# First attention of a two-layer kernel: causal mask of the transposed scores by a minimum on VectorE instead of mask matmuls on TensorE

## What is computed

```
attn = jnp.einsum('bhqd,bhkd->bhqk', q, k) / math.sqrt(HEAD_DIM)
attn = attn + alibi_bias(seq_len, N_HEADS)[None] + causal_mask(seq_len)[None, None]
attn = jax.nn.softmax(attn, axis=-1)
y = jnp.einsum('bhqk,bhkd->bhqd', attn, v)
x = x + (y @ W_o) * silu(ffn(xn))      # written short; the FFN has a Walsh-Hadamard transform
```

## Time and profile before

| | |
|---|---|
| median of three runs | 1381.1 us |
| profiled execution, span from first to last instruction | 1408.8 us |
| TensorE matmuls busy | 1272.3 us |
| VectorE busy | 846.9 us |
| ScalarE busy | 597.1 us |
| GpSimd busy | 473.7 us |
| mean granted TensorE clock | 0.965 |
| first layer | about 18 to 455 us of the span |

### The profile page before, as it was taken

The page is one execution under the profiler, slowest core; times in us unless marked ns, Lnnn a source line. Parts: engine busy times, 40 slices in busy tenths (PEclk is TensorE's granted clock), DMA queues, the critical chain, the costliest instruction groups (busy, mean ns, idle before and its releaser), DMA issues.

```text
span 1408.8 us, 26582 instructions
## 1 busy us (share of the span) xinstructions
PE 1272.3 (90%) x9326; PEld 1107.9 (79%) x9327; DVE 846.9 (60%) x1731; ACT 597.1 (42%) x1351; POOL 473.7 (34%) x488
## 2 busy tenths in 40 slices
PE   5699979979998879989897899899999999999996
PEld 4588878768777766667666888889998999898996
DVE  4647547557556553333346777767665676667685
ACT  3333323323323334444453444454554555455542
POOL 0112332332331320000007878644343444343442
PEclk9799999999999999999999999999999999999998
DMA  5744314223101943323223121200000000000001
GB/s 196 282 177 154 134 59 150 100 97 143 46 31 36 340 174 94 93 82 97 89 76 116 53 76 46 75 1 31 2 1 31 1 31 1 1 1 1 1 24 38
DMA packets 63658, 112.07 MB, mean 80 GB/s; under 512 B 6977, under 2 KB 36033, under 8 KB 62017
## 3 DMA queue, kind: packets, MB, share of 16 engines
q1 hardware_dynamic: 57408, 93.79, 19.0%
q0 software_dynamic: 6144, 16.79, 3.6%
HBM read 49.86 MB, written 60.69 MB: 78 GB/s over the span
## 4 chain that ended last, share of the span: by engine, by line
PE 80%; DVE 8%; issue 7%; ACT 3%; POOL 1%; DMA 1%; another core or an unknown queue 1%; SPq 0%; ACTq 0%; DVEq 0%; POOLq 0%
PE bank L705 7%; PE six L722 6%; PE six L830 4%; PE bank L792 4%; PE bank L794 4%; PE bank L793 4%; PE bank L392 4%; PE bank L393 3%; PE bank L394 3%; PE bank L867 2%; PE bank L865 2%; PE bank L866 2%; PE bank L804 2%; PE six L844 2%; PE bank L805 2%
## 5 line engine op out<-in xcount | busy, mean ns | idle before, releaser
L1822 POOL TENSOR_TENSOR rstd<-msq,half_pow 128x8 f32<-128x8 f32 x64 | 105.5, 1648 | 163.1 <-DVE msq L1633 162.7
L1149 ACT ACTIVATE pT<-six,rstd 128x256 f32<-128x256 f32 x128 | 60.9, 476 | 213.6 <-PE six L831 213.6
L1759 POOL TENSOR_TENSOR hid_l<-hid,hid_h 128x256 fp32r<-128x256 f32 x64 | 48.2, 753 | 243.4 <-ACT hid_h L963 243.4
L1834 POOL TENSOR_TENSOR pT<-pT,tri_mul 128x512 f32<-128x512 f32 x64 | 84.3, 1318 | 130.8 <-ACT pT L1195 129.9
L1233 DVE TENSOR_TENSOR yT1l<-six,yT1h 128x512 fp32r<-128x512 f32 x64 | 44.3, 692 | 135.0 <-ACT yT1h L1200 135.0
L705 PE MATMUL bank<-experts,xT 128*128 x316 | 109.5, 470 | 17.5 <-issue 16.8
L1626 DVE TENSOR_TENSOR sq<-xs 128x512 f32<-128x512 f32 x128 | 102.1, 797 | 23.3 <-ACT xs L1168 23.3
L792 PE MATMUL bank<-bw_h,xT1h 128*128 128x512 f32 x256 | 106.9, 418 | 6.5 <-issue 6.5
L794 PE MATMUL bank<-bw_l,xT1h 128*128 128x512 f32 x256 | 101.8, 398 | 0.0
L793 PE MATMUL bank<-bw_h,xT1l 128*128 128x512 f32 x256 | 101.1, 395 | 0.0
L830 PE MATMUL six<-qT,kT 128*128 128x256 f32 x256 | 78.5, 388 | 18.7 <-issue 15.4
(11 more groups left out here) (282 smaller groups left out, 4068.4 us busy)
## 6 DMA issues: line engine op xcount, KB each, us to landing
cells_scratch<-zeros SPq DMA_DIRECT2D x8, 4352.0 KB, 14.9
xg<-cells_scratch SPq DMA_DIRECT2D x79, 128.0 KB, 2.0
cells_scratch<-y SPq DMA_DIRECT2D x79, 128.0 KB, 1.7
experts<-pack_experts_dram SPq DMA_DIRECT2D x16, 608.0 KB
raw<-pack_attn_dram SPq DMA_DIRECT2D x8, 1024.0 KB, 4.9
raw<-pack_w_dram SPq DMA_DIRECT2D x2, 1024.0 KB, 4.8
xT_scratch<-xT1h_c SPq DMA_DIRECT2D x8, 256.0 KB, 2.0
xT_scratch<-xT1l_c SPq DMA_DIRECT2D x8, 256.0 KB, 2.6
```

The source lines that it names most:

```text
L1822: pool.tensor_tensor(out=rstd[:, r, :], in0=msq[:, r, :], in1=half_pow[:], op=ALU.pow).then_inc(rstd_sb, 1)
L1834: pool.tensor_tensor(out=p, in0=p, in1=tri_mul[:].unsqueeze(1).unsqueeze(1).to_broadcast([P, 2, 2, P]), op=ALU.mult).then_inc(masked1, 1)
```

## The change

`scores_T` loses its four mask matmuls; its score matmuls now start their banks themselves. A new VectorE step `causal(b, g)` takes the minimum of the two diagonal blocks of each head with `tri_cap`, in place in PSUM, in two instructions of two heads each (128 x 512). `tri_cap` is fp32, 1e30 where the key may be seen and -1e30 where not. `exps` waits for the half it reads instead of for `scores_T`. `causal` is called at four places of VectorE's batch.

```diff
-                for h in range(GH):
-                    pe.matmul(six[:, h, 0:T], ident_b[:], tri_addT[:].rearrange("p c k -> p (c k)"),
-                              start=True, stop=False, skip_group_check=True)
                 for h in range(GH):
                     r = slice(h * VW, (h + 1) * VW)
-                    pe.matmul(six[:, h, P:3 * P], kA[r, g, 0:P], qB[r, g, :], start=False, stop=True, skip_group_check=True)
+                    pe.matmul(six[:, h, P:3 * P], kA[r, g, 0:P], qB[r, g, :], start=True, stop=True, skip_group_check=True)
                 for h in range(GH):
                     r = slice(h * VW, (h + 1) * VW)
-                    last = pe.matmul(six[:, h, 0:P], kA[r, g, P:T], qB[r, g, P:T], start=False, stop=True,
+                    last = pe.matmul(six[:, h, 0:P], kA[r, g, P:T], qB[r, g, P:T], start=True, stop=True,
                                      skip_group_check=True)
                 last.then_inc(sT0_ps, 1)
...
             def exps(b, g):
-                act.wait_ge(sT0_ps, 4 * b + g + 1)
                 after(act, y0_ps, 4 * b + g - 1)
                 for h in (0, 2):
+                    act.wait_ge(causal0, 8 * b + 2 * g + h // 2 + 1)
                     last = act.activation(pT0[:, g % 2, h:h + 2, :], six[:, h:h + 2, 0:3 * P], ACT.Exp)
                 last.then_inc(exp0, 1)
...
+            def causal(b, g):
+
+                dve.wait_ge(sT0_ps, 4 * b + g + 1)
+                for h in (0, 2):
+                    s = six[:, h:h + 2, 0:T].rearrange("p h (c q) -> p h c q", c=2)
+                    dve.tensor_tensor(out=s, in0=s, in1=tri_cap[:].unsqueeze(1).unsqueeze(1).to_broadcast([P, 2, 2, P]),
+                                      op=ALU.min).then_inc(causal0, 1)
...
                 if not first:
                     out_T(t)
+                    causal(b, 0)
                     gate_s(t, banks[0][:, :])
                 if first:
+                    causal(b, 0)
                     ffn_lo(2, w1_l, w1_h)
                     ffn_lo(3, w3_l, w3_h)
...
                 hidden(b, 1)
                 beside(3)
+                causal(b, 1)
                 if not first:
                     stats(t, st1, mv1, ve1, st1_sb, mv1_sb, ve1_sb, b)
...
                 hidden(b, 3)
                 heads_out(b, 1)
+                causal(b, 2)
                 if not final:
                     stats(b + 1, st0, mv0, ve0, st0_sb, mv0_sb, ve0_sb)
...
                 hidden(b, 5)
                 heads_out(b, 2)
+                causal(b, 3)
                 if not first:
                     router(t, 0)
...
-            dve.tensor_scalar(out=tri_addT[:], in0=tri_mul[:].unsqueeze(1).to_broadcast([P, 2, P]), scalar1=1.0,
-                              scalar2=1e30, op0=ALU.subtract, op1=ALU.mult)
+            dve.tensor_scalar(out=tri_cap[:], in0=tri_mul[:], scalar1=0.5, scalar2=2e30, op0=ALU.subtract, op1=ALU.mult)
```

More of the change, by code:

```diff
@@ L103, in build @@
         hadamard_r = sa("hadamard_r", [P, P], F32R)
-        ident_b, tri_add, tri_addT = sa("ident_b", [P, P], BF16), sa("tri_add", [P, 2, P], BF16), sa("tri_addT", [P, 2, P], BF16)
+        ident_b, tri_add, tri_cap = sa("ident_b", [P, P], BF16), sa("tri_add", [P, 2, P], BF16), sa("tri_cap", [P, P])
         q_row, k_rows = sa("q_row", [P, 1]), sa("k_rows", [P, NG, T])
@@ L198, in build @@
             "down_ps"))
-        yt0_sb, yq0_ps = sem("yt0_sb"), sem("yq0_ps")
+        yt0_sb, yq0_ps, causal0 = sem("yt0_sb"), sem("yq0_ps"), sem("causal0")
         xT1_ps, lgT_ps, lg_ps, pos_ps = (sem(n) for n in ("xT1_ps", "lgT_ps", "lg_ps", "pos_ps"))
@@ L441, in scores_T @@
                 for h in range(GH):
-                    pe.matmul(six[:, h, 0:T], ident_b[:], tri_addT[:].rearrange("p c k -> p (c k)"),
-                              start=True, stop=False, skip_group_check=True)
+                    r = slice(h * VW, (h + 1) * VW)
+                    pe.matmul(six[:, h, P:3 * P], kA[r, g, 0:P], qB[r, g, :], start=True, stop=True, skip_group_check=True)
                 for h in range(GH):
                     r = slice(h * VW, (h + 1) * VW)
-                    pe.matmul(six[:, h, P:3 * P], kA[r, g, 0:P], qB[r, g, :], start=False, stop=True, skip_group_check=True)
-                for h in range(GH):
-                    r = slice(h * VW, (h + 1) * VW)
-                    last = pe.matmul(six[:, h, 0:P], kA[r, g, P:T], qB[r, g, P:T], start=False, stop=True,
+                    last = pe.matmul(six[:, h, 0:P], kA[r, g, P:T], qB[r, g, P:T], start=True, stop=True,
                                      skip_group_check=True)
```

## The result

The changed kernel took 1395.97 us (median of 4 runs, 1395.54 to 1396.85), the kernel before 1377.95 us on the same chip (4 runs, 1373.42 to 1381.57): ratio 1.0134, 95% interval [1.0101, 1.0168]. It is slower, by 18 us where 9.6 were forecast; the time lies in the forecast's range of 1377 to 1404 us.

The account below looks back on a forecast made before the run. TensorE was taken as the bound by a few tenths only, VectorE in batch 0; 3 x 0.5 + 1.0 + 3 x 1.4 + 2.9 = 9.6 us slower made 1391 us, range 1377 to 1404.

Parts of the forecast that it names:

- the chain: First attention, each group: the minimum between scores_T and the exponentials ends them about 0.7 us later; likeliest case, slower, chance 0.44.
- The halves: The two VectorE minimum instructions per group: 0.69 us each, starting when VectorE leaves hidden(1) or heads_out(1), not at scores_T's end.
- PE waits before L421 of groups 2 and 3: TensorE before the scores of groups 2 and 3: idle 0.5 to 0.7 us, released by ScalarE's exponentials.
- maxima_T: TensorE's L435 behind maxima(2) in group 1: L1288 and L1289 end late, so it waits 0.3 us.
- The router's path: Group 3: r_th comes 0.5 us later, delaying hidden(6); TensorE's wait before norm_T0 grows from 0.93 to near 1.5 us.
- The ordinary batch: Batches 1, 3 and 5: each 0.5 us longer, not 1.8 shorter.
- Batch 0: First batch, VectorE-bound by butterflies: hidden(2) 3.1 us late, passed on to the hadamard matmul; less 0.2, +2.9 us.
- The held batches: Batches 2, 4, 6 and 7, with VectorE waiting on "remote": +1.0 us in batch 2, +1.4 in each other.
- rival A: Whole kernel: no difference that can be told, within 6.9 us; with weaker holds 6.4 us more, 1387.5; chance 0.34.
- Rival B: TensorE in the first attention: faster, its time returns as exponentials stay covered; at most 14.7 us, 1366; chance 0.10.
- Rival D: TensorE after the wait before norm_T0: clock falls, 1.6 us in each of six batches, 10 more, 1401; chance 0.12.
- The base: Whole kernel: traced span 1408.8 us is 27.7 above the runs' 1381.1; this difference was carried over to the forecast.

Follow-up runs that it names:

- e8: The changed kernel itself, unedited, traced again on one chip with the kernel before: 1415.80 us, ratio 1.0062 to the kernel before.
- e9: The kernel before, unedited, traced again on the same chip as the changed kernel: 1406.36 us, ratio 0.9991.
- e10: The kernel before without any mask (no matmuls, no minimum; exponentials scaled by 0.25) and with TensorE's batch loop written out: 1382.90 us, ratio 0.9843.
- e5: The kernel before with TensorE's loop over batches 1 to 6 written out, mask matmuls kept: 1396.45 us, ratio 0.9897 to the kernel before.
- e0: The kernel before, unedited, run for a second profile: 1396.86 us, ratio 1.000.
- e2: The changed kernel with the mask matmuls put back beside the minimum: 1421.30 us, ratio 1.0136 to the kernel before.
- e1: The kernel before without any mask (no mask matmuls, no minimum; exponentials scaled by 0.25), loop kept: 1396.72 us, ratio 0.9985.
- e3: The changed kernel with VectorE's order changed in batch 0 alone, causal(1) ahead of the last butterflies: 1414.50 us, ratio 1.0108 to the kernel before.
- e6: No mask matmuls or minimum; VectorE multiplies the exponentials by a triangle in SBUF, loop kept: 1403.99 us, ratio 0.9979 to the kernel before.
- e11: The changed kernel, unedited, run a third time on a third chip: 1414.53 us, ratio 1.0076 to the kernel before.

## Why the prediction was right, and where it was short

**The sign and the chain: right.** The steps it named show in the rows above. The instruction is 0.69 us. The halves start at the end of hidden(1) and of heads_out(1). PE waits before L421 of groups 2 and 3 in batches 1 to 7, 0.43 to 0.49 in each, for 0.5 to 0.7 forecast. maxima_T waits 0.20 for 0.3. The router's path, the step that passes the rest to the end of the batch (compare):

```profile
281.07 0.65 PE L402 MATMUL bank<-ident,xn 128*128 128x128 f32 x4 [1.65 <-DVE hid L1312]
```

is 1.65 for "near 1.5". The ordinary batch is 0.30 longer, forecast 0.5.

**Batch 0: right.** Timeline of DVE, ACT and PE, against the earlier trace rows:

```profile
40.63 1.29 DVE L1301 TENSOR_TENSOR six<-six,tri_cap 128x512 f32<-128x512 f32 x2
41.36 1.51 ACT L939 ACTIVATE pT<-six 128x768 f32<-128x768 f32 x2 [3.69 <-DVE six L1301]
43.48 0.42 DVE L1308 SCALAR_TENSOR_TENSOR th<-th,bank 128x256 f32<-128x256 f32 x1 [1.56 <-ACT th L955]
...
50.95 0.80 PE L606 MATMUL bank<-w_h,hadamard_r 128*128 128x512 f32 x1 [11.98 <-DVE w_l L1230]
```

DVE is idle for the forecast's 1.6 us (1.56) behind exps(1). Counted from the first scores, the hadamard matmul is 2.9 us later in e8 than in e9 (50.29 - 18.22 against 48.22 - 19.05), and the batch 3.1; between the two first traces it is 2.0 and 2.3.

**The held batches: near in sum where there are holds, not one by one.** Without the jumps' longer waits, batches 2, 4, 6 and 7 gave 0.95, 1.28, 1.00 and 0.62 for 1.0, 1.4, 1.4 and 1.4 in the pair e8 and e9. Batches 3 and 5 gave 2.1 and 0.0 for 0.5. They were taken as ordinary, but they have holds in these traces (PE waits 2.90 us for qA before L520 in batch 3 of e8), and had them in the trace of before, where the prediction looked only at DVE's gate:

```profile
196.43 0.61 PE L442 MATMUL six<-tri_addT,ident_b 128*128 128x256 bf16 x4 [3.57 <-issue]
...
305.66 0.61 PE L442 MATMUL six<-tri_addT,ident_b 128*128 128x256 bf16 x4 [3.69 <-issue]
```

The holds move between executions; a price per batch isn't to be had from one. That 9.35 comes so near to 9.6 is in part luck: batch 5's 0.0 holds 1.4 us of a slow start that e9 had and e8 had not. And the changed kernel's own trace, on the chip of the result, has no hold in any of batches 2 to 7. There the chain can be estimated as batch 0's 3.1 and 7 x 0.3, some 5 us, near rival A's 6.4 for a kernel with weak holds.

**What was missing: the jump.** The sum ran over groups and batches and took PE's loop as free. The trace of before had its wait, and it was not read as something that a change of PE's code can move:

```profile
186.11 0.61 PE L421 MATMUL six<-tri_add,ident_b 128*128 128x256 bf16 x4 [2.38 <-issue]
...
295.23 0.61 PE L421 MATMUL six<-tri_add,ident_b 128*128 128x256 bf16 x4 [2.35 <-issue]
```

It became 5.1 to 5.8 each: +5.5 us for the two in the pair e8 and e9, which with the chain's 9.35 makes 14.9. Rival B's mechanism (PE's time comes back) is real too, 11.3 of 14.7 us in e10 against e5; with the loop the jumps eat a good part of it, and with the minimum the exponentials' delay eats the rest.

**Rival D (the clock) was near in the price, 1.6 us for 1.4 to 2.9, and wrong about the place.** After the 1.65 us of idle time before norm_T0 the clock stays up: the changed kernel's batches 1 and 6, with that wait in them, have 1.00 granted:

```profile
88.00:136.00 48.00, 44.80 (x473) 39.06 (x466) 37.12 (x89) 17.48 (x37) 8.46 (x11) 1.00 0.29 105
344.40:392.50 48.10, 44.72 (x470) 39.03 (x466) 36.92 (x89) 17.49 (x37) 16.36 (x19) 1.00 0.10 34
```

It falls after the jumps' 2.4 to 5.8 us, in both kernels, at every jump but one (e0's second, after 2.60 us), and behind the holds. The Trainium skill ("TensorE: Matmul & The Clock Gate", section "What's actually happening") calls the throttled clock the default state, which activity releases. The traces agree with it at 19 of 20 jumps; at norm_T0 1.65 us of idle time brought no lower clock.

**The base.** The prediction carried over 27.7 us between before's span and its runs and took them for the profiler's. They are not: in e0, in e9 and in the changed kernel the span lies 1.8 to 1.9 us under that execution's own time. Before was traced in an execution with holds: its first attention took 439.0 us, the changed kernel's without holds 424.0. An estimate for before without holds is 424.0 less 5 for the chain and 7 for the jumps (6 of waiting, 1 of slow start), 412, which is 27 less than traced and agrees with the 27.7. So the runs on the result's chip were probably without holds, or with few; no profile caught the kernel before near 1378, and why a chip has them in nearly every run and another doesn't isn't settled.

So the sum had two faults that partly met: it priced holds that the chip of the result most likely didn't have (9.6 where 5 are estimated), and it left out the jumps. Of the measured 18 us, the estimate accounts for 5 + 7 = 12. The other 6 are open; four experts' turns at the lower clock would make them, and the changed kernel's trace has seven such turns. That 1391 came within 5 us of 1396 is in part luck. What is shown is the sign, the chain's steps and the jumps' longer waits.

## What to carry to other kernels

When work is taken from the busiest engine, look at who hands it the next operand: here 0.46 us per group came off TensorE and 0.7 went in front of the exponentials it waits for. The same mask behind the exponentials, with as many VectorE instructions, takes 1.3 us less a batch.

Price the loop as well as its body. An idle time that nothing releases at a loop's turn can move with the code: here it went from 2.4 to 2.9 us to 5.1 to 5.8 when 32 matmuls left the loop. In one stage of six batches, writing the loop out made the traces 5 to 13 us shorter, and in the kernel before it gained 1.0% (0.6 to 1.4), more than any change of the mask did. And before a few us are credited to an edit, look at the stretches it doesn't touch for turns at another clock.

## What the runs showed of the hardware

**At a jump one or two packets of instructions arrive.** The DMA view of PE's idle time at the jump, the queue of instruction packets (packets, MB, share of the 16 engines). The changed kernel, 182.0 to 188.5:

```profile
q8 instruction: 2, 0.03, 2.4%
```

The kernel before (e9), 181.0 to 184.3:

```profile
q8 instruction: 1, 0.02, 1.8%
```

Each packet is 16,384 bytes. The first starts within 0.4 us of PE running dry; where there is a second it starts 3.0 to 3.5 us behind the first, and L421 starts 2.3 to 3.0 us after the last one. This holds at all 20 jumps of the ten traces with a loop: one packet and 2.35 to 2.93 us in the four with the mask matmuls (before, e0, e9, e2), two and 5.12 to 5.83 us in the six without (the change, e1, e3, e6, e8, e11). In the written-out kernels packets arrive too, while PE works, and L421 of batches 3 and 5 has no wait. The likely reading is that the shorter code puts the loop's start so near the end of a packet that its first matmuls lie in the next one. That PE waits for the packets, and this, is argued from the rows; a kernel with only the start moved (a few empty instructions in front) wasn't run.

**"remote" holds are late signals.** In the trace of before, PE's signals to DVE and ACT arrive 1.0 to 5.3 us after the matmul that gives them has ended, while GpSimd issues its indirect transfers (L1768). They are what the earlier trace rows show as waits for "remote". PE then stands idle 1.3 to 3.7 us in each of batches 2 to 7. Every trace has such late signals but one: in the changed kernel's first trace GpSimd issues the same eight transfers in each batch, over 10 us as before, and no signal of PE's is late by 0.8 us. So the transfers alone don't make a hold; what else it takes is open.

**The experts' slow turns begin behind a jump too.** In e9 the five slow turns each have 1.2 GHz granted from 1.1 to 1.4 us after L705 has started (a granted clock of 1.00 from 644.3 to 645.6, 0.51 from 645.6 to 648.9, 1.00 from 649.1), behind the 1.95 to 1.98 us that PE waited at the loop's turn; in the fast turns the same wait brings no lower clock. What decides between the two isn't shown.
